# Norms' roots moved to POOL, a norm ahead of its weights, and two MLPs in three split products

## What is computed

```python
def layernorm(x, scale, bias):
    m = jnp.mean(x, axis=-1, keepdims=True)
    v = jnp.mean(jnp.square(x - m), axis=-1, keepdims=True)
    return (x - m) * jax.lax.rsqrt(v + EPS) * scale + bias
...
ln_out = layernorm(x, ln3_s, ln3_b)
mlp_out = gelu(ln_out @ w1 + b1) @ w2 + b2
return x + mlp_out
```

## Time and profile before

| | |
|---|---|
| runs | 2299.34, 2298.61, 2294.14 us; median 2298.61 |
| the profiled execution | 2292.91 us, its span 2291.2 us |
| TensorE's granted clock, mean | 0.955 of full |
| busy share: PE / PEld / DVE / ACT / POOL | 90 / 72 / 41 / 44 / 29 % |
| chain that ended last, by engine | PE 78, ACT 8, DVE 7, issue 3, POOL 3, DMA 1 % |
| instructions | 37962 |

### The profile page before, as it was taken

One profiled execution on the slowest core, in us unless ns is written; L12 is line 12 of the kernel. 1 busy time (PEld: TensorE's weight loads), 2 busy tenths in 40 slices (PEclk: granted clock), 3 DMA queues, 4 the chain that ended last, 5 costly groups with the idle time before them and its releaser, 6 DMA issues.

```text
span 2291.2 us, 37962 instructions
## 1 busy us (share of the span) xinstructions
PE 2064.6 (90%) x15565; PEld 1638.6 (72%) x15565; DVE 946.5 (41%) x1758; ACT 1000.0 (44%) x2605; POOL 656.4 (29%) x768
## 2 busy tenths in 40 slices
PE   7878788896899999999899999999988987878799
PEld 4555566664788888888788888888855666666566
DVE  3443223204444444445444444443311177776510
ACT  3322444453343443434343344434344367666622
POOL 2311202104132231413224132221121067666500
PEclk9977898998999999999999999999999989999999
DMA  4000000001000000000001000000020010000000
GB/s 136 10 6 2 6 1 1 1 1 42 28 19 19 10 29 1 28 1 19 1 19 47 1 29 10 10 1 1 1 84 1 16 32 1 6 1 6 2 19 19
DMA packets 28174, 38.36 MB, mean 17 GB/s; under 512 B 1744, under 2 KB 19808, under 8 KB 28000
## 3 DMA queue, kind: packets, MB, share of 16 engines
q1 hardware_dynamic: 28000, 35.93, 4.9%
HBM read 33.83 MB, written 2.10 MB: 16 GB/s over the span
## 4 chain that ended last, share of the span: by engine, by line
PE 78%; ACT 8%; DVE 7%; issue 3%; POOL 3%; DMA 1%; SPq 0%; DVEq 0%; ACTq 0%; POOLq 0%
PE ps L184 34%; PE ps L2137 5%; PE ps_four L2283 5%; PE ps_four L2303 5%; PE ps_four L2121 4%; PE ps L2121 3%; PE ps_four L2292 2%; ACT l_pt L1502 2%; PE ps_four L2051 2%; PE ps L2179 2%; POOL l_sm L1352 1%; PE ps L2110 1%; PE ps L2089 1%; PE ps L2097 1%; PE ps L2313 1%
## 5 line engine op out<-in xcount | busy, mean ns | idle before, releaser
L1596 ACT ACTIVATE l_prob<-ps_four,l_mx 128x129 f32<-128x129 f32 x512 | 181.4, 367 | 593.9 <-DVE l_mx L1896 593.9
L1386 POOL TENSOR_TENSOR l_prob<-l_prob,l_mx 128x516 f32<-128x516 f32 x128 | 134.1, 1048 | 782.8 <-DVE l_mx L1903 782.8
L184 PEld LDWEIGHTS ps<-l_wo,l_ao 128*128 128x128 f32 x1536 | 198.8, 190 | 20.8 <-DVE l_ao L1915 6.8
L184 PE MATMUL ps<-l_wo,l_ao 128*128 128x256 f32 x1536 | 206.0, 283 | 5.5 <-DVE l_ao L1915 5.5
L184 PE MATMUL ps<-ctxT,l_wk 128*128 128x512 f32 x768 | 210.3, 409 | 0.0
L184 PE MATMUL ps<-l_hT,l_wq 128*128 128x512 f32 x768 | 210.1, 409 | 0.0
L184 PE MATMUL ps<-l_wv,ctxT 128*128 128x512 f32 x768 | 202.9, 400 | 0.3
L1352 POOL TENSOR_TENSOR l_sm<-l_sm,l_mask 128x1024 f32<-128x1024 f32 x64 | 150.2, 2368 | 132.6 <-DVE l_sm L1861 132.4
L184 PEld LDWEIGHTS ps<-l_wv,ctxT 128*128 128x128 f32 x768 | 142.6, 189 | 42.9 <-ACT l_qT L1577 8.3
L1825 DVE TENSOR_TENSOR x_tok<-x_tok,ps 128x512 f32<-128x512 f32 x98 | 63.5, 684 | 237.2 <-PE ps L2137 177.0
L184 PEld LDWEIGHTS ps<-ctxT,l_wk 128*128 128x128 f32 x768 | 135.7, 190 | 23.1
(11 more groups left out here) (232 smaller groups left out, 3830.8 us busy)
## 6 DMA issues: line engine op xcount, KB each, us to landing
l_staging<-in_L_xattn_wv SPq DMA_DIRECT2D x8, 512.0 KB, 3.6
l_staging<-in_L_xattn_wk SPq DMA_DIRECT2D x8, 512.0 KB, 3.7
l_staging<-in_L_xattn_wq SPq DMA_DIRECT2D x8, 512.0 KB, 4.1
l_staging<-in_L_xattn_wo SPq DMA_DIRECT2D x8, 512.0 KB, 3.8
x_tok<-in_x SPq DMA_DIRECT2D x4, 512.0 KB, 7.5
ctx_tok<-in_ctx SPq DMA_DIRECT2D x4, 512.0 KB, 5.9
l_mlp_w<-in_L_xattn_mlp_w SPq DMA_DIRECT2D x2, 1024.0 KB, 8.7
l_w<-in_L_xattn_w_fc SPq DMA_DIRECT2D x2, 1024.0 KB, 6.5
```

Of the source, the lines that this page charges most:

```text
L184: ins = e.matmul(out, a, b, start=start and i == 0, stop=stop and i == 2, skip_group_check=not check)
L1386: e.tensor_tensor(pr[:, :, 0:S + 1], pr[:, :, 0:S + 1], mx[:, 3, :].unsqueeze(2).to_broadcast([P, GB, S + 1]), ALU.mult).then_inc(sem("poo ...
L1596: ins = e.activation(pr.t[:, b, 0:S + 1], banks[b // 2].t[:, (b % 2) * (S + 2):(b % 2) * (S + 2) + S + 1], ACT.Exp, bias=mx[:, 1, b:b + 1] ...
```

## The change

There are four parts.

1. **Roots.** `norm_rstd` leaves ACT. VectorE adds eps to the variance (in the RMS norm within the addition that was there), and POOL raises the 128x4 tile to the power -0.5 by a TENSOR_TENSOR with a constant tile. 28 norms do so; with them the table loads in the program fall from 53 to 35.
2. **Rows.** Beside the MLPs of layers three and four the rows are made by VectorE's `norm_xn`; in the attention of layer four they stay on ACT.
3. **Layer three's first norm** is put ahead of its weights: its statistics are mixed with those of layer two's last norm, and then its stages and those of the weights take turns.
4. **MLPs of layers three and four** multiply in three products (`mlp_split`). VectorE splits the weights once per layer (`mlp_w`), the normalised and transposed input once per group (`mhs`, one buffer), and for the hidden slice ACT runs the gelu twice, once into the hi half and once in place in the PSUM bank, from which VectorE subtracts hi to give lo (`hid3`, two buffers). Per k TensorE does 6 matmuls of 512 and 12 of 256 columns; down(k-2) is planned behind up(k). The slack and the rates of mixing change with it. The new tiles share their space with buffers of the attention, so the weights of layer four's MLP are split only when its last units are done: w1 and the input before the last products of the attention, w2 behind them.

```diff
+L3_MLP2_SLACK, L3_MLP2_RATES = 12, (5.0, 9.5, 9.5)
+L3_MLP3_SLACK, L3_MLP3_RATE = 4, 2.3
...
+def alternate(first, other):
+    for _ in first:
+        yield next(other, None)
+    yield from other
...
+    def mlp_input(self, u, m, hs_done):
+
+        pl = self.pl
+        yield from pl.until(self.mhs)
+        pl.slot(self.mhs, "mhs", m)
+        for c in range(DC):
+            pl.emit("mhs", m, c, src=u, src_done=hs_done)
+            yield
+        pl.free(*u, by=("dve.mhs", m, DC - 1))
...
+    def mlp_split(self, m, phase, b1, func):
+
+        pl = self.pl
+        self.mlps[m] = dict(phase=phase, b1=b1, func=func, down="pe.down3")
+        for k in range(FC + 2):
+            if k < FC:
+                yield from pl.until(self.misc)
+                pl.bank(self.misc, "up3", m, k)
+                pl.emit("up3", m, k)
+            if k == FC - 1:
+                pl.free("mhs", m, by=("full", "up3", m, k))
+            if k == 2:
+                for i in range(2):
+                    yield from pl.until(self.side)
+                    pl.bank(self.side, "side", m, i)
+            if k >= 2:
+                pl.emit("down3", m, k - 2)
+                pl.free("hid3", m, k - 2, by=("pe.down3", m, k - 2))
+                yield
+            if k < FC:
+                pl.slot(self.hid3, "hid3", m, k)
+                pl.emit("hid3", m, k)
+                pl.free("up3", m, k)
...
-        interleave(until_norm(self.l1_last), chain(load_weights(0, 0), normalise(0, 0)), 2.5)
+        first, weights = normalise(0, 0), load_weights(0, 0)
+        for _ in range(5):
+            next(self.l1_last)
+            next(first)
+        interleave(until_norm(self.l1_last), alternate(first, weights), 2.5)
...
-        run(norm2(0))
-        interleave(mlp2(0), chain(norm2(1), self.load_weight("l3_w_kv", a["L3_xattn_w_kv"], "pool")), 1.2)
...
-        interleave(mlp2(1), chain(begin(0), values("a", 0), norm2(2)), 2.2)
-        interleave(mlp2(2), chain(begin(1), values("a", 1), norm2(3)), 2.2)
-        run(mlp2(3))
...
+            self.xn_stage = "dve.norm_xn"
+            first, weights = norm2(0), self.mlp_weights("l2m", ("sp.l2m_plain", 32))
+            for stages, n in ((first, 7), (weights, 2)):
+                for _ in range(n):
+                    next(stages)
+            run(first)
+            self.slack = L3_MLP2_SLACK
+            interleave(mlp2(0), chain(weights, norm2(1), self.load_weight("l3_w_kv", a["L3_xattn_w_kv"], "pool")), L3_MLP2_RATES[0])
...
+            interleave(mlp2(1), chain(begin(0), values("a", 0), norm2(2)), L3_MLP2_RATES[1])
+            interleave(mlp2(2), chain(begin(1), values("a", 1), norm2(3)), L3_MLP2_RATES[2])
+            run(mlp2(3))
...
+        self.xn_stage = "act.norm_xa"
...
-        run(rest)
+        attention.close()
+        probs_done, over_done = ("full", "four", "l3", N - 1, 1), ("full", "over", "l3", N - 1)
+        self.mlp_tiles("l3e", scope, (probs_done, over_done, ("pool.l3_scores", N - 1)))
+        weights = self.mlp_weights("l3e", ("sp.l3_mlp", 32))
+        for _ in range(2):
+            next(weights)
+        run(self.mlp_input(("hs", ("l3n", 3, 0)), ("l3e", 0), h_done["l3e", 0]))
+        interleave(rest, weights, 1.0)
+        self.xn_stage = "dve.norm_xn"
...
-        self.slack = 0
+        self.slack = L3_MLP3_SLACK
         for g in range(G):
-            interleave(mlp3(g), norm3(g + 1) if 1 <= g < G - 1 else iter(()), 1.2)
+            interleave(mlp3(g), norm3(g + 1) if 1 <= g < G - 1 else iter(()), L3_MLP3_RATE)
...
+        def norm_rstd(u):
+
+            nm = self.norms[u]
+            rs = nm["st"]["rs"]
+            q.wait_ge(*pl.done("dve.norm_var", u))
+            if nm["last"] is not None:
+                q.wait_ge(*pl.done(self.norms[nm["last"]]["xn_stage"], nm["last"], 1))
+            e.tensor_tensor(rs[:, 4, :], rs[:, 3, :], self.minus_half[:], ALU.pow).then_inc(sem("pool.norm_rstd"), 1)
...
-            table(ACT.Ln)
-            e.activation(rs[:, 3, :], rs[:, 1, :] if nm["rms"] else mv[:, :, 1], ACT.Ln, bias=self.eps[:, i:i + 1]).then_inc(
-                sem("act.norm_rstd:l"), 1)
-            q.wait_ge(*pl.done("act.norm_rstd:l", u))
-            e.activation(rs[:, 4, :], rs[:, 3, :], ACT.Exp, scale=-0.5).then_inc(sem("act.norm_rstd"), 1)
...
+        def hid3(m, k):
+
+            f, bk, hid = self.mlps[m], use["up3", m, k], use["hid3", m, k]
+            q.wait_ge(*pl.event(("full", "up3", m, k)))
+            q.wait_ge(*pl.event(hid.before))
+            table(f["func"])
+            e.activation(hid.t[:, 0, :], bk.t, f["func"], bias=f["b1"][:, k:k + 1])
+            e.activation(bk.t, bk.t, f["func"], bias=f["b1"][:, k:k + 1]).then_inc(sem("act.hid3"), 1)
...
-                ins.then_inc(sem("dve.norm_var"), 1)
+                self.rms += 1
+                q.wait_ge(sem("dve.norm_rms"), self.rms)
+                if nm["last"] is not None:
+                    q.wait_ge(*pl.done("pool.norm_rstd", nm["last"]))
+                e.tensor_scalar(rs[:, 3, :], mv[:, :, 1], nm["eps"], None, ALU.add).then_inc(sem("dve.norm_var"), 1)
...
+        def mlp_w(phase, name, part):
+            f, src = pl.info["mlp_w", phase, name, part], self.l3_w[name]
+            c = src.shape[1] // 2
+            cs = slice(part * c, (part + 1) * c)
+            hi, lo = (half[:, cs] for half in self.mlp_halves(phase, name))
+            q.wait_ge(sem(f["landed"][0]), f["landed"][1])
+            q.wait_ge(*pl.event(self.mlp_w[phase, name][1]))
+            e.tensor_copy(hi, src[:, cs]).then_inc(sem("dve.mlp_w:hi"), 1)
+            q.wait_ge(*pl.done("dve.mlp_w:hi", phase, name, part))
+            e.tensor_tensor(lo, src[:, cs], f32(hi), ALU.subtract).then_inc(sem("dve.mlp_w"), 1)
...
+            e.tensor_copy(hi, src).then_inc(sem("dve.mhs:hi"), 1)
+            q.wait_ge(*pl.done("dve.mhs:hi", m, c))
+            e.tensor_tensor(lo, src, f32(hi), ALU.subtract).then_inc(sem("dve.mhs"), 1)
...
+        def hid3(m, k):
+            bk, hid = use["up3", m, k], use["hid3", m, k].t
+            q.wait_ge(*pl.done("act.hid3", m, k))
+            e.tensor_tensor(hid[:, 1, :], bk.t, f32(hid[:, 0, :]), ALU.subtract).then_inc(bk.slot.empty, 1)
...
+        def up3(m, k):
+            f = self.mlps[m]
+            w, hs = self.mlp_halves(f["phase"], "w1"), [use["mhs", m].t[:, i] for i in range(2)]
+            q.wait_ge(*pl.done("dve.mlp_w", f["phase"], "w1", 1))
+            q.wait_ge(*pl.done("dve.mhs", m, DC - 1))
+            bk = fill("up3", m, k)
+            for c in range(DC):
+                ins = matmul_split(e, bk.t, [half[:, c, k * P:(k + 1) * P] for half in w], [half[:, c, :] for half in hs],
+                                   c == 0, c == DC - 1)
+            ins.then_inc(bk.slot.full, 1)
+
+        def down3(m, k):
+            f, hid = self.mlps[m], [use["hid3", m, k].t[:, i, :] for i in range(2)]
+            w = self.mlp_halves(f["phase"], "w2")
+            q.wait_ge(*pl.done("dve.mlp_w", f["phase"], "w2", 2 * k // FC))
+            q.wait_ge(*pl.event(("empty", "up3", m, k)))
+            banks = [fill("side", m, i) for i in range(2)]
+            for b in range(GB):
+                ins = matmul_split(e, banks[b // 2].t[:, (b % 2) * D:(b % 2 + 1) * D], [half[:, b * S:(b + 1) * S] for half in hid],
+                                   [half[:, k, :] for half in w], k == 0 and b % 2 == 0, k == FC - 1, check=False)
+            ins.then_inc(sem("pe.down3"), 1)
```

111 lines of the change are left out of this document (68 added, 43 removed).

## The result

| | before | changed |
|---|---|---|
| median of the runs | 2295.72 us (6 runs, 2291.8 to 2299.3) | 2288.95 us (6 runs, 2288.5 to 2289.6) |
| ratio | 1 | 0.997, 95% interval 0.9957 to 0.9983 |
| profiled execution, span | 2291.2 us | 2287.8 us |

Of the 27 us that were forecast, 6.8 came. Beside the runs of a later job the changed kernel stood at 2292.25 against 2295.65, ratio 0.9986 (0.9974 to 0.9998). By these two results the change makes the kernel faster by 0.14 to 0.3%, and the two intervals together reach from 0.02 to 0.43%. The first result lies just outside the range of 2256 to 2288, and its gain just under the 6.9 us (0.3%) that the prediction called the least that can be told from none.

What follows compares the result with a forecast made beforehand. TensorE, busy 90% of the span, was taken as the bound. MLPs of layers three and four -8.2 and -13.3, attention +2, boundary -7.5: -27.0 us, so 2271.6 against the 2298.6 median; range 2256 to 2288.

Steps and rivals of the forecast that it cites:

- the boundary: Entry to layer three, 520 to 580 us, up to its first scores: TensorE's hole shrinks, -7.5 us (-12 to +3).
- att. 3 and the front: Layer three's attention, and all up to layer two's last output-weight matmul: forecast at 0 each.
- signs of being wrong: A power row over 1 us, waits inside a group, or layer four's 337 us attention growing by more than 5.
- Roots on POOL: Layer four's attention: roots queue behind POOL's waiting score rows, +2 us (0 to +10); a power taken as 0.2 to 0.4.
- the wait behind wo: Entry to layer three: the second norm's root queues on POOL behind wk, wq and wo, holding TensorE's transposes, +4.3 us.
- the hold at kT: At 577.91 us a table load and root hold kT and TensorE for 3.37 us; leaving ACT was to give -1.8.
- Layer three's MLP: Products -17.3 us, entry +7, w2's split and statistics ahead of a hid slice +2.8, norms and group ends -0.7: -8.2.
- The entry: Ahead of layer three's MLP TensorE waits for VectorE's split of w1 and the input: +7 us (+5 to +14).
- layer four's MLP: Products -17.3 us, group ends and one bare input split +4.0, entry hidden behind the attention: -13.3.
- rival (d): Both MLPs: each split matmul takes half of f32's record, a k 2.58 us; -46 us, 2252; chance 0.04.
- Rival (a): Slower: powers on POOL; each us beyond 0.3 costs 19, gain gone from 1.4 more; at 2.2, 2313; chance 0.04.
- Rival (b): Gain mostly eaten: contended VectorE, entry +14, no gain at the boundary, attention +5; -11.5 us, 2287; chance 0.18.

Runs made afterwards that it cites:

- e2: The changed kernel with only the eight roots of layer four's attention back on ACT: 2285.85 us, ratio 0.9965.
- e6: The changed kernel with a multiplication in place of the power in layer four's attention (wrong root there): 2289.21 us, ratio 0.9961.
- e7: The changed kernel with roots on POOL only beside the MLPs of layers three and four, on ACT elsewhere: 2269.3 us, ratio 0.9879; repeated, 2271.67 us.
- e8: The changed kernel with the MLPs of layers three and four in f32 again: 2306.19 us, ratio 1.0038.
- e9: The kernel with roots on POOL only beside both MLPs, with layer three's MLP back in f32: 2269.58 us, ratio 0.988.
- e1: The changed kernel with all 28 roots back on ACT: 2281.81 us, ratio 0.9956.
- e5: The changed kernel with the product -mean x root in layer four's attention made by POOL instead of VectorE: 2299.84 us, ratio 1.0032.
- e10: The kernel with roots on POOL only beside both MLPs, with half of layer three's w1 split on POOL: 2271.95 us, ratio 0.9894.

## Why the prediction was wrong

In the profiles -27.0 became -3.2 up to the last matmul: 14.6 of the missing 23.8 us stand in layer four's attention, 7.0 at the boundary and 5.3 in att. 3 and the front, while entry and MLPs give 3.1 back. Two of the prediction's own signs of being wrong came: power rows over 1 us, and an attention stretch that grew by more than 5.

**The step that failed** is "Roots on POOL": "the eight norms of that stretch are planned with slack ... +2 (0 to +10)". Measured were 12.5 us for these eight (353.6 against 341.1 in e2), over the upper end, and 16.6 for the stage. I had named the cause rightly, a root that waits behind a wait, and then priced it with the power's own duration and trusted a slack of two plan steps. One step isn't a time: in the norm shown above two score rows, 4.68 us, fit into it. And I looked only at who needs the root for the norm, not at what stands behind the waiting instruction: VectorE's product holds the unit's maximum, and with it the ring. e6 says that the length was about a quarter of it; had the power been as short as a copy, the term would still have been 7 to 8 short.

**The boundary** was forecast at -7.5 and gave -0.5. Its parts: the MLP went on 8.0 us earlier instead of 10 (counted from the end of the front), the wait behind wo cost 5.5 instead of 4.3, the slow clock behind it 2.9 that the sum had at nothing, and the hold at kT shrank by 0.9 instead of 1.8. With the roots off POOL the same order gives -8.3 (55.7 in e7). So moving the norm does most of what the sum said, and the roots took it away again. Set against e7, part by part, the 7.8 us are 0.5 by the restart of the MLP (two powers, 2.0 us, stand ahead of wv's first half), 5.5 by the wait behind wo, 2.9 by the clock, and 1.0 back at kT, where e7 has its table load again. What I overlooked besides is that POOL now waits 3.9 us for wk and 4.5 for wq to land, where before the splits ran without a gap; that the rows, which hold buffers of the staging ring, delay these loads is my reading and wasn't tried. In e7 the same waits (3.9 and 4.8) cost TensorE nothing, since no root stands behind them.

**Layer three's MLP** was right as a sum, but divides otherwise by experiment. Forecast was -17.3 for the products, +2.8 once, and -0.7 for norms and group ends; measured, e8 gives -11.7 for rows, roots and slack alone, and the split -6.2 on top. In e8 the norms' waits are gone, as their 8.9 us promised; in the changed kernel 4.1 of them remain (2.4 for the norms' rows, 1.7 for the attention parts), and the stalls of the split are waits of their own: 3.4 for the input split, twice, and 2.6 for hid slices, of which 1.2 at w2. These 10.1 us stood in the sum as 11.0 (8.2 and 2.8), and the products' 17.3 were 19.8 at the measured 2.82 a k. The stalls should have stood against the product's saving: then it would have been plain that layer three's three products pay for nothing but their own entry (+8.3), which e9 confirms.

**The entry** (+7 forecast, +7.9) and **layer four's MLP** (-13.3 forecast, -14.6; entry hidden, last input split ready 2 us ahead) came out as worked.

**Matmul rates.** Up 1.38 and down 1.44: the trace's rows carried over, a little better than 2.90 in all. The estimate of 2.60 from the gap of N/2.4+2.5 ns that the Trainium skill gives (TensorE: Matmul & The Clock Gate, Back-to-back issue gap), and rival (d) with it, is refuted: no run shows a k under 2.82.

**Rival (a)**, the root on POOL, had a chance of 0.04 and was the mechanism, 12.5 us at the attention and 7.8 at the boundary: 20 over its 19 roots, 1.1 each and under its point of decision of 1.4. I had put the mechanism's whole weight on slower results and none on the middle. Rival (b) came nearest in its result (2287), partly by luck: its second term, a boundary that gains nothing because of the root behind wo, is what happened; the 7 us that it added at the entry were 1, and its +5 in the attention were 12.5. Its sum also has 5.5 for the boundary where its text has 7.5; with 7.5 it gives 2289.

**What stays open.** With no root on POOL in it, the attention of layer four still takes 341 to 347 us instead of 337. Neither the split MLP ahead (e9) nor the roots (e1, e2) explain it; VectorE's eight additions of eps and the tiles that share space were not tried apart. Against e1 the kernel before lacks in this stage just these eight additions and, at its end, the eight instructions that split w1 and the input; and with one profile of before and a stage that moves by 4 to 5 us with unchanged instructions, part of the gap may be no more than that. Nor is the 4 us in att. 3 settled, for which there is one profile of before; kernels with and without roots on POOL there read alike (1089.0 to 1090.9 but for two at 1094). In the front, the seven profiles with roots on POOL read 520.5 on average (517.1 to 525.5), the six of experiments with roots on ACT 516.7 (513.1 to 522.4): too scattered to put a price on four roots. And in e2, e5 and e8 the median of the runs is itself some 6 to 9 us above what the stages from the boundary on, with front and att. 3 as in the other kernels, would give: a trait of these builds, in front or att. 3, that nothing here explains. Deeper rings for hid and the input split weren't tried.

## What to carry to other kernels

When an operation moves to another engine's in-order queue, price the instruction that is planned just ahead of it there and the one that stands behind its reader, not the operation: eight powers of 1 us cost 12.5, and most of it stayed with operations of 0.2 us. A wait of TensorE can also cost more than its length: 5.4 us at the boundary brought 2.9 more at the lower clock. The same move can pay in one stage and cost in another: on POOL the roots saved 13 us beside layer three's MLP, where ACT has the gelus, and lost 20 where POOL's queue was full, and choosing by stage (e7) gave more than either placement did throughout. A matmul form that saves on every product must also pay for its split: ask per stage, since here it gave 14.7 us where the split was hidden and nothing where it stood at the entry.

## What the runs showed of the hardware

- A TENSOR_TENSOR power of 128x4 on POOL took 1007 to 1028 ns (median 1017) in all 28 places of the changed kernel; a multiplication of the same tiles 205 ns, a copy 191.
- VectorE beside POOL: a 128x512 cast of 0.43 us took 2.56 beside POOL's 128x1024 addition, a 128x512 subtraction of 0.69 took 2.71 (e10), and POOL's own operation went from 2.35 to 3.32. Splitting w1 between the two engines in the same microseconds gained nothing (e10, entry 20.7 instead of 19.7).
- Split matmuls of 512 columns ran at 0.23 us each and those of 256 at 0.12 in both MLPs, at a granted clock of 1.00.
- After a hole TensorE ran on at the lower of its two clock levels for a while: behind 9.50 us without work the granted clock was 0.50 (1.2 of 2.4 GHz) for the next 5.25 us, and split matmuls of 512 columns took 0.44 us each; behind 5.37 us it was 0.60 over the next 7.18, and an up of 1.88 us in f32 took 3.62.
- Layers one and two wander by 8 us between profiles with the same instructions. Up to 500 us the granted clock of a stretch of 50 us lies between 0.74 and 1.00 and differs between profiles (350 to 400 us: 0.81 in e2 and e5, 0.88 in the changed kernel), while from 600 to 1600 us it is 0.97 to 1.00 in stretches of 100 us.
